# GpSimd's order turned, low halves of weights on VectorE, eight result buffers, x and results laid by query, masks and x loaded first

## The reference

```python
def _L0_xattn_ref(input, memory, mask, w_input, dot_scale):
    input_dot = jnp.einsum('bqd,od->bqo', input, w_input)
    cross_dot = jnp.einsum('bqd,bkd->bqk', input * dot_scale, memory)
    att = input_dot + cross_dot - 1e+30 * mask[:, None, :]
    return jnp.einsum('bqk,bkd->bqd', jax.nn.softmax(att, axis=-1), memory)

def _moe_forward(x, W_router, W_gate, W_up, W_down):
    probs = jax.nn.softmax(jnp.einsum('bsd,ed->bse', x, W_router), axis=-1)
    gates, indices = jax.lax.top_k(probs, 2)
    gates = gates / jnp.sum(gates, axis=-1, keepdims=True)
    # for each expert: y = (silu(x wg) * (x wu)) wd, out += weight * y

x = x + jnp.tanh(g_xattn[0]) * _L0_xattn_ref(_layernorm(x), ctx_1024, mask, w_input, dot_scale)
x = x + jnp.tanh(g_ffn[0]) * _L0_ffn_ref(_layernorm(x), W_router, W_gate, W_up, W_down)
```

## Time and profile before

| | |
|---|---|
| runs | 308.25, 307.16, 308.09 us, median 308.09 |
| profiled execution | 306.35 us, of which the span 304.6 |
| PE busy | 251.2 us, 82% |
| PE weight loads | 205.2 us, 67% |
| VectorE (DVE) | 129.4 us, 42% |
| ScalarE (ACT) | 137.3 us, 45% |
| GpSimd (POOL) | 141.8 us, 47% |
| DMA | 39.27 MB, mean 129 GB/s |

### The profile page before, as it was taken

One profiled execution on the slowest core, in us unless ns is written; L12 is line 12 of the kernel. 1 busy time (PEld: TensorE's weight loads), 2 busy tenths in 40 slices (PEclk: granted clock), 3 DMA queues, 4 the chain that ended last, 5 costly groups with the idle time before them and its releaser, 6 DMA issues.

```text
span 304.6 us, 5760 instructions
## 1 busy us (share of the span) xinstructions
PE 251.2 (82%) x1598; PEld 205.2 (67%) x1599; DVE 129.4 (42%) x421; ACT 137.3 (45%) x295; POOL 141.8 (47%) x243
## 2 busy tenths in 40 slices
PE   5957978999879998798899449739999999999910
PEld 4635758777667776676597438627988888888710
DVE  0252455656535565259446306272334243333205
ACT  2345546555455554555264304412555454545400
POOL 3072432444685666787855885640332323232320
PEclk9997997999989999799979959976999999999975
DMA  5996885778737888479851301321111111114027
GB/s 135 205 194 186 219 201 141 181 171 197 190 109 177 192 214 240 123 208 229 267 171 37 80 8 38 80 64 35 47 43 45 39 49 36 50 39 150 17 73 276
DMA packets 21246, 39.27 MB, mean 129 GB/s; under 512 B 3830, under 2 KB 14134, under 8 KB 21222
## 3 DMA queue, kind: packets, MB, share of 16 engines
q1 hardware_dynamic: 17334, 34.29, 43.7%
q0 software_dynamic: 2560, 3.77, 4.2%
q10 hardware_dynamic: 1328, 0.92, 1.0%
HBM read 32.87 MB, written 6.09 MB: 128 GB/s over the span
## 4 chain that ended last, share of the span: by engine, by line
PE 52%; POOL 15%; DMA 11%; ACT 8%; issue 8%; SPq 3%; DVE 3%; POOLq 0%; DVEq 0%
PE psum L1100 8%; PE psum L997 7%; PE psum L977 7%; PE psum L1078 6%; PE psum L1080 5%; PE psum L1079 5%; DMA maskb<-mask_scaled 5%; PE psum L1089 4%; PE psum L964 4%; DMA x_all<-in_x 4%; POOL slots L528 3%; POOL w_lo L502 3%; ACT probs L650 3%; ACT probsT L616 2%; PE psum L987 2%
## 5 line engine op out<-in xcount | busy, mean ns | idle before, releaser
L583 POOL DMA_INDIRECT results<-y_sb,dest x32 | 30.7, 959 | 65.3 <-DVE dest L897 52.6
L997 PE MATMUL psum<-ctx_sb,probsT 120*100 120x128 f32 (+1 forms) x384 | 51.7, 290 | 0.0
L997 PEld LDWEIGHTS psum<-ctx_sb,probsT 120*100 120x100 f32 (+1 forms) x384 | 47.3, 180 | 0.2 <-issue 0.2
L502 POOL TENSOR_TENSOR w_lo<-w_raw,w_hi 128x512 fp32r<-128x512 f32 x16 | 20.3, 1269 | 50.2 <-ACT w_hi L627 50.0
L977 PE MATMUL psum<-ctxT,qT 128*100 128x512 f32 (+1 forms) x96 | 42.8, 582 | 0.2 <-issue 0.2
L908 DVE SCALAR_TENSOR_TENSOR scores<-probs,row_in,psum 128x512 f32<-128x512 f32 x32 | 23.9, 747 | 38.2 <-ACT probs L682 36.7
L682 ACT ACTIVATE probs<-psum 128x512 f32<-128x512 f32 x32 | 19.1, 597 | 45.7 <-PE psum L1080 40.9
L528 POOL DMA_INDIRECT slots<-pair_rows,slot_i x32 | 33.2, 1036 | 9.8 <-issue 8.5
L1100 PE MATMUL psum<-w_down,hidT 128*128 x256 | 35.8, 285 | 1.0 <-ACT y_sb L694 0.6
L754 DVE CUSTOM_DVE_ANT_0 scores<-psum,maskb 100x1444 f32<-100x1444 f32 x16 | 26.6, 1660 | 18.9 <-PE psum L977 11.7
L1100 PEld LDWEIGHTS psum<-w_down,hidT 128*128 128x128 f32 x256 | 32.7, 200 | 1.8 <-issue 1.8
(11 more groups left out here) (126 smaller groups left out, 371.2 us busy)
## 6 DMA issues: line engine op xcount, KB each, us to landing
ctx_sb<-in_ctx SPq DMA_DIRECT2D x16, 720.0 KB
maskb<-mask_scaled SPq DMA_DIRECT2D x14, 564.1 KB
w_raw<-in_w_experts SPq DMA_DIRECT2D x16, 256.0 KB
row_in<-slots SPq DMA_DIRECT2D x32, 65.0 KB, 1.8
w_down<-in_w_experts SPq DMA_DIRECT2D x4, 512.0 KB
maskb<-in_mask SPq DMA_DIRECT2D x2, 564.1 KB
x<-x_all SPq DMA_DIRECT2D x2, 400.0 KB
ctx_sb<-x SPq DMA_DIRECT2D x1, 800.0 KB, 4.5
```

The costliest lines, as they stand in the source:

```text
L502: nc.gpsimd.tensor_tensor(w_lo[:, b * WC:(b + 1) * WC], w_raw[:, b % 2, :], w_hi[:, b * WC:(b + 1) * WC].bitcast(F32), ALU.subtract).then_ ...
L583: nc.gpsimd.indirect_dma_start(results, bass.IndirectOffsetOnAxis(ap=dest[:, s:s + 1], axis=0), y_sb[:, s, :], None).then_inc(y_stored[s], 16)
L997: last = nc.tensor.matmul(attn_ps[0:Q, 0:D], probsT[0:rows[c], c, :], ctx_sb[0:rows[c], b % RING, c, :], start=(c == 0), stop=(c == CHUNKS ...
```

## The change

- `split_weights` moves from POOL to VectorE, where part b-2 is split in step b ahead of the masked maximum. ScalarE rounds part b-1 in step b, two in step 15, and `w_raw` has four buffers instead of two.
- On POOL the rows of batch 14 come ahead of the gates of batches 12 and 13, and the first result is scattered ahead of the rows of batches 14 and 15.
- `y_sb` and `dest` have eight buffers (`YRING`), and the loop does eight tiles a turn.
- x comes in laid out by query, in groups (0,2), (2,4), (4,8), (8,12), (12,16). Results are laid by query; they are added onto `x_all` itself in four groups of four batches, and stored from there. `x2` is gone, with two stores and a load.
- SP's order: before step 0 there are x to batch 7, context 0 to 2 and the two raw masks. Step b then issues mask b+2, weights b, context b+3; context 3 comes in step 0 behind mask 2, the last two groups of x in steps 1 and 2, and the store of the empty rows in step 3.
- Ten warming matmuls instead of eight at the start.

```diff
-        X_GROUPS = [(0, 1), (1, 4), (4, 8), (8, 12), (12, 16)]
+        X_GROUPS = [(0, 2), (2, 4), (4, 8), (8, 12), (12, 16)]
...
-                wait(sp, w_lo_done, b - 1)
-                sp.dma_start(w_raw[:, b % 2, :], w_experts[:, b * WC:(b + 1) * WC]).then_inc(w_loaded[b % 2], 16)
+                wait(sp, w_lo_done, b - RING + 1)
+                sp.dma_start(w_raw[:, b % RING, :], w_experts[:, b * WC:(b + 1) * WC]).then_inc(w_loaded[b % RING], 16)
...
             load_raw_mask(1)
-            load_weights(0)
+            load_x(2)
             load_ctx(2)
-            load_x(2)
-            load_weights(1)
-            load_ctx(3)
-            load_x(3)
-            sp.wait_ge(empty_done, 1)
-            sp.dma_start(slots[DUMMY:DUMMY + P, :], empty[:, :]).then_inc(empty_stored, 16)
-            load_x(4)
 
             for b in range(B - 2):
                 sp.wait_ge(scores_done, b + 1)
                 if b == 0:
                     sp.wait_ge(mask_stored, 16)
                 load_mask(b + 2)
-                load_weights(b + 2)
-                if b + RING < B:
-                    sp.wait_ge(attn_raw, b + 1)
-                    load_ctx(b + RING)
-                if b == 8:
-                    store_x2(0, 8)
+                if b == 0:
+                    load_ctx(RING - 1)
+                load_weights(b)
+                if 1 <= b and b + RING - 1 < B:
+                    sp.wait_ge(attn_raw, b)
+                    load_ctx(b + RING - 1)
+                if b in (1, 2):
+                    load_x(b + 2)
+                if b == 3:
+                    sp.wait_ge(empty_done, 1)
+                    sp.dma_start(slots[DUMMY:DUMMY + P, :], empty[:, :]).then_inc(empty_stored, 16)
                 if b >= 10:
                     load_down(b - 10)
+            load_weights(B - 2)
+            load_weights(B - 1)
...
+                sp.dma_start(out[m * CUT:(m + 1) * CUT, :, :].rearrange("b q d -> q b d"),
+                             x_all[:, m * CUT:(m + 1) * CUT, :]).then_inc(out_stored, 16)
...
-                if b == B - 1:
-                    split_weights(b)
                 if b in SCATTERS:
...
-                if b < B - 1:
-                    split_weights(b)
...
-            gates(12, 14)
             root2(B - 2)
             normalise2(B - 2)
+            gates(12, 14)
             root2(B - 1)
             normalise2(B - 1)
             pool.wait_ge(placed, 7)
             scatter(12)
             scatter(13)
             gates(14, 16)
-            pool.wait_ge(placed, 8)
-            scatter(14)
-            scatter(15)
...
                 scatter_result(0, n)
+                if n == 0:
+                    pool.wait_ge(placed, 8)
+                    scatter(14)
+                    scatter(15)
...
-                    round_weights(b)
+                    if b >= 1:
+                        round_weights(b - 1)
+                    if b == B - 1:
+                        round_weights(B - 1)
...
+            def split_weights(b):
+                dve.wait_ge(w_hi_done, b + 1)
+                apart(dve)
+                nc.vector.tensor_tensor(w_lo[:, b * WC:(b + 1) * WC], w_raw[:, b % RING, :],
+                                        w_hi[:, b * WC:(b + 1) * WC].bitcast(F32), ALU.subtract).then_inc(w_lo_done, 1)
...
                     attention_gain(b - 1)
+                if b >= 2:
+                    split_weights(b - 2)
+                if b == B:
+                    split_weights(B - 1)
                 if b < B:
                     masked_max(b)
...
-                    wait(dve, y_stored[s], i * 16 + 16 * (k // RING))
-                    nc.vector.tensor_tensor(dest[:, s:s + 1], row_in[:, s, D + 1:D + 2], spare[:, s:s + 1], ALU.min).then_inc(dest_done, 1)
+                    o = k % YRING
+
+                    wait(dve, y_stored[o], i * 16 + 16 * (k // YRING))
+                    nc.vector.tensor_tensor(dest[:, o:o + 1], row_in[:, s, D + 1:D + 2], spare[:, o:o + 1], ALU.min).then_inc(dest_done, 1)
...
+                part = x_all[:, m * CUT:(m + 1) * CUT, :]
                 dve.wait_ge(first_loaded[m], 16)
-                nc.vector.tensor_tensor(x2_sb[:, cut], x2_sb[:, cut], first_sb[:, cut], ALU.add).then_inc(first_added, 1)
+                nc.vector.tensor_tensor(part, part, first_sb[:, m * CUT:(m + 1) * CUT, :], ALU.add).then_inc(first_added, 1)
...
-            keep_warm(8)
+            keep_warm(10)
```

More of the change, by code:

```diff
@@ L27 @@
 RING = 4
-LAG = 3
+YRING = 8
 NEG = -1e30
@@ L215, in build @@
         ctx_loaded = [sem(f"ctx_loaded{s}") for s in range(RING)]
-        w_loaded = [sem(f"w_loaded{s}") for s in range(2)]
+        w_loaded = [sem(f"w_loaded{s}") for s in range(RING)]
         down_loaded = sem("down_loaded")
@@ L284, in build @@
         y_done = sem("y_done")
-        y_stored = [sem(f"y_stored{s}") for s in range(RING)]
+        y_stored = [sem(f"y_stored{s}") for s in range(YRING)]
         first_loaded = [sem(f"first_loaded{m}") for m in range(CUTS)]
@@ L306, in over_tiles @@
                     after(n)
-            with eng.Fori(0, (LOOP_END - LOOP) // RING) as i:
-                for k in range(LOOP, LOOP + RING):
+            with eng.Fori(0, (LOOP_END - LOOP) // YRING) as i:
+                for k in range(LOOP, LOOP + YRING):
                     step(i, k)
@@ L401, in _ @@
             sp.wait_ge(scattered[0], 16 * 2 * PARTS[EARLY_PART][1])
-            for n in range(RING):
-                load_rows(0, n)
-            store_x2(8, B)
-            for n in range(RING, LOOP):
+            for n in range(LOOP):
                 load_rows(0, n)
@@ L410, in _ @@
                         clear_tail(e)
-            with sp.Fori(0, (LOOP_END - LOOP) // RING) as i:
-                for k in range(LOOP, LOOP + RING):
+            with sp.Fori(0, (LOOP_END - LOOP) // YRING) as i:
+                for k in range(LOOP, LOOP + YRING):
                     load_rows(i, k)
@@ L587, in _ @@
                 scatter_result(0, n)
-            with pool.Fori(0, (LOOP_END - LOOP) // RING) as i:
-                for k in range(LOOP, LOOP + RING):
+                if n == 0:
+                    pool.wait_ge(placed, 8)
+                    scatter(14)
+                    scatter(15)
+            with pool.Fori(0, (LOOP_END - LOOP) // YRING) as i:
+                for k in range(LOOP, LOOP + YRING):
                     scatter_result(i, k)
@@ L871, in _ @@
             statistics1(0)
+            statistics1(1)
             dve.wait_ge(scale_loaded, 32)
             evict_ctxT(0)
-            for b in range(1, 4):
-                statistics1(b)
+            statistics1(2)
+            statistics1(3)
             dve.wait_ge(mask_raw, 16)
@@ L917, in add_results @@
             def add_results(m):
-                cut = slice(m * CUT, (m + 1) * CUT)
+                part = x_all[:, m * CUT:(m + 1) * CUT, :]
                 dve.wait_ge(first_loaded[m], 16)
-                nc.vector.tensor_tensor(x2_sb[:, cut], x2_sb[:, cut], first_sb[:, cut], ALU.add).then_inc(first_added, 1)
+                nc.vector.tensor_tensor(part, part, first_sb[:, m * CUT:(m + 1) * CUT, :], ALU.add).then_inc(first_added, 1)
                 dve.wait_ge(second_loaded[m], 16)
                 dve.wait_ge(first_added, m + 1)
-                nc.vector.tensor_tensor(x2_sb[:, cut], x2_sb[:, cut], second_sb[:, cut], ALU.add).then_inc(second_added, 1)
+                nc.vector.tensor_tensor(part, part, second_sb[:, m * CUT:(m + 1) * CUT, :], ALU.add).then_inc(second_added, 1)
             rowT_low(0, 0)
@@ L1092, in down @@
             def down(i, k):
-                n = i * RING + k
+                n = i * YRING + k
                 o = k % 2
@@ L1155 @@
     laid = {
-        "x": a["x"],
+        "x": a["x"].transpose(1, 0, 2),
         "ctx": a["ctx_1024"],
```

100 lines of the change are left out of this document (42 added, 58 removed).

## The result

The kernel after took 288.53 us (median of 4 runs, 287.06 to 290.59), the kernel before beside it 307.62: ratio 0.939, interval 0.932 to 0.946. Predicted were 282.5 us, range 275 to 291. On chip 6 the same two kernels later gave 280.79 and 305.51 us, ratio 0.920 (0.914 to 0.926).

What follows compares the result with a forecast made beforehand. PE was taken to set the pace of undisturbed attention steps, with late POOL, loads and SP's clears adding waits. Terms -3.7 - 11.8 - 7.7 - 1.2 - 1.5 + 1.4 = -24.5 from 306.35 gave 281.9, predicted as 282.5 us, range 275 to 291.

Steps and rivals of the forecast that it cites:

- start, to maximum 4: From the start to maximum 4: new load order brings mask 2 earlier but x late; -3.7 us (0 at worst).
- attention, maximum 4 to 15: Masked maxima 4 to 15: long steps fall back to 8.33 us, 105.6 becomes 93.8; -11.8 us (bounds -14 and -4).
- maximum 15 to tile 0: Last masked maximum to first expert tile: rows 14 ready sooner, 10.0 for 17.72 us; -7.7 us (bounds -5 and -9).
- tile 0 to 7: First seven expert tiles: SP's clears still late, buffers buy nothing before tile 6; -1.2 us (0 to -3).
- loop: Expert loop: turns of eight and fewer waits for stores save time; -1.5 us (0 to -2.5).
- last copy to end: Results by query at the end: additions +1.0 us, last store +0.4, loads nothing; +1.4 us (0.5 to 2.5).
- POOL's wait was the price: Attention: the split's 4.69 us wait for ScalarE makes POOL late; without it long steps fall back to 8.33 us.
- The backlog of step 10: POOL's 10.0 us of work in step 10 makes rows 9 and query 13 late: 1.1 us of PE idling.
- Who is held up: VectorE's new subtraction may hold up POOL's roots and rows, 0.70 us each time; 0.65 charged for two steps.
- The rival of transfers as the bound: Attention steps take 9.1 us for 1.54 MB of transfers, eleven steps lose 8.5, total 291 us; chance 0.15.

Runs made afterwards that it cites:

- experiments 1 and 2: Kernel after with the split back on POOL: at its old place with the wait, 300.88 us (0.982); one part later without it, 287.8 us (0.944).
- clears_late: Kernel after with the index-tail clears issued behind the row load of tile 7 instead of ahead of tile 6's; 290.35 us, ratio 0.937.
- yring4: Kernel after with four result buffers and turns of four tiles instead of eight; 290.16 us, ratio 0.949.
- flat_x2: Kernel after with the old end, x2 to memory and results by batch over 128 partitions; 279.43 us, ratio 0.908.
- experiment 3: Same run as flat_x2: kernel after with the old end, results by batch over 128 partitions; 279.43 us, ratio 0.908.
- clears_two: Kernel after with four of the eight index-tail clears issued from ScalarE's queue; 280.80 us, ratio 0.918.
- tail96: Kernel after with each load of results at the end cut into 96 and 4 queries; 282.69 us, ratio 0.925.
- 6: Kernel after with the fourth part of x issued before the first step instead of behind weights 1; 293.06 us, lowest of four 286.11.
- 8: Kernel after with each mask loaded in two transfers, of 96 and 4 queries; 284.12 us, ratio 0.926.
- 7: Same run as clears_late: kernel after with the index-tail clears behind the row load of tile 7; 290.35 us, ratio 0.937.
- 10: Same run as clears_two: kernel after with four of the eight clears on ScalarE's queue; 280.80 us, ratio 0.918.
- experiment 5: Same run as yring4: kernel after with four result buffers and turns of four instead of eight; 290.16 us, ratio 0.949.

## Why the prediction was right, and where not

The sum by steps, in us against the profiled execution of before (there is no trace of the kernel before from the other chip, so that column carries that chip's own speed too):

| step | predicted | after | other chip |
|---|---|---|---|
| start, to maximum 4 | -3.7 | -3.6 | -0.3 |
| attention, maximum 4 to 15 | -11.8 | -9.4 | -14.0 |
| maximum 15 to tile 0 | -7.7 | -6.6 | -8.0 |
| tile 0 to 7 | -1.2 | -0.2 | -4.7 |
| loop | -1.5 | -2.1 | -1.7 |
| last copy to end | +1.4 | +4.5 | +4.9 |
| sum | -24.5 | -17.3 | -23.8 |

The sum on the other chip is near the forecast by luck: the start gained 3.4 us less than forecast and the end cost 3.5 more, while attention gained 2.2 more and the tiles 3.5 more.

- *POOL's wait was the price.* Shown by experiments 1 and 2, with what stands queued behind it. The split takes 0.69 us on VectorE (0.70 predicted) and delayed no maximum. The backlog of step 10 is there: at 111.49 POOL comes to the roots of batch 9's rows straight from its gates.
- *Who is held up.* I feared it for POOL's roots and rows, and it is so. L438 takes 0.19 us alone, and 0.44 to 0.49 in ten steps in which it starts inside VectorE's subtraction; it then ends with the subtraction. L437 mostly slips in ahead with 0.22 to 0.23 us and was caught twice (0.82 us at 93.10, 0.76 at 118.99). VectorE's own 0.68 to 0.69 never grew. The steps of 8.17 and 8.41 us are those of the undisturbed steps of before, so where POOL has time it costs nothing.
- *Attention.* The seven steps came as said (58.1 us in six of the seven executions named here, 59.8 in `clears_late`). The term as a whole is too small by some 2.5 us on average: 93.8 predicted, 96.2 and 91.6 measured, and 92.1, 96.0, 98.4, 99.1 and 100.5 in `yring4`, `flat_x2`, `clears_two`, `tail96` and `clears_late`, whose attention is the same (`flat_x2` has one store more). What scatters most is the last four steps: 33.5 and 34.0 us at 230 and 226 GB/s, 37.9 at 220, 38.1 at 206, 40.3 and 40.6 at 197, 40.9 at 194, for 7.7 to 8.3 MB each (length times rate). The three longest stand in executions of 283.8, 296.6 and 286.8 us, where the fastest of those kernels took 278.3, 286.1 and 278.9. In the first execution PE waited 2.79 us for context 14, which landed 14.48 us after its issue; share 0.82 there at 206 GB/s, 0.86 at 230 on the other chip. The rival of transfers as the bound is thus true in part, in four steps and some executions. What sets the rate in an execution stays open.
- *Start.* x was there at 42.5 (43 forecast), and the time was met, but the step named one cause where there are two. ScalarE was held 6.71 us by weights 0 (2 to 4 forecast). The new split stands ahead of the maximum on VectorE and waited 5.46 us for ScalarE, where nothing was charged for it, so maximum 2 came at 35.48 instead of near 32. With x in front nothing was gained (6); with weights 0 sooner VectorE waited longer for x (8). That fits the bytes of the whole order as the limit. Maximum 4 stood between 52.3 and 56.8 in the eight executions that share this start, so meeting -3.7 is luck; on the mean of the eight it is -2.
- *End of attention.* 10.0 predicted, 11.14 and 9.73 measured. In the 11.14 PE waited 0.22 us for rows 14, its last wait before tile 0 but a short one; on the other chip none shows.
- *Tile 0 to 7.* SP's clears set it, and the eight buffers bought nothing, as forecast (5, 7, 10). The clears' own duration differs (12.49 and 8.11 us), which is nearly the whole difference of 4.5.
- *Loop.* 1.5 predicted, 2.1 and 1.7 measured; experiment 5 puts 1.5 on buffers and turns together.
- *The failed step is the last.* "The eight additions grow from 400 columns to 512 ... The last store leaves in 512-byte pieces": I charged +1.4 and it was +4.5. Issue of the loads, first and last addition, before (the last stands in the earlier trace rows) and after:

```profile
294.45 1.75 SPq L422 DMA_DIRECT2D ctx_sb<-results  x4
...
297.52 0.58 DVE L921 TENSOR_TENSOR ctx_sb<-ctx_sb 128x400 f32<-128x400 f32 x1 [10.25 <-DMA ctx_sb<-results]
```

```profile
272.64 1.56 SPq L408 DMA_DIRECT2D ctx_sb<-results  x4
...
277.08 0.69 DVE L914 TENSOR_TENSOR x_all<-x_all,ctx_sb 100x512 f32<-100x512 f32 x1 [11.63 <-DMA ctx_sb<-results]
...
283.22 0.69 DVE L917 TENSOR_TENSOR x_all<-x_all,ctx_sb 100x512 f32<-100x512 f32 x1 [0.47 <-DVE x_all L914]
```

The additions were 0.69 us as said (+0.9). The load of the results was put at nothing: the first addition starts 4.44 us after the issue instead of 3.07 (+1.4), and later ones wait again (+1.2). From the end of the last addition to the end of the span it is 3.39 us instead of 2.32, +1.1 where 0.4 was charged for the store. The mechanism (the layout by query costs at the end) was right, its size a third. That the loads over 100 partitions take 0.61 of the DMA engines was seen only in the trace after; that masks go to 100 partitions too could be read before, but no row of before shows such a transfer alone.

The 3.1 us of that step, 2.4 of attention, 1.1 before tile 0, 1.0 in the tiles and 0.1 at the start, less 0.6 of loop, are the 7.2 by which the sum missed (each rounded).

## What to carry to other kernels

Cost an in-order engine's wait by what stands queued behind it, not by the instruction: 1.27 us of subtraction cost 4% only with the wait in front. When a layout changes, price its loads and stores and not only the arithmetic: results over 100 partitions instead of 128 cost 3.4 to 3.9 us where nothing hides it, of which the longer additions were 0.9. And before a miss of 1 to 2% is explained, or one stretch of one trace is used against a theory, run the same kernel again, on another chip too: the same four steps took 33.5 to 40.9 us.

## What was not expected of the hardware

- The same kernel took 288.5 us on one chip and 280.8 on another (0.939 and 0.920 of the kernel before). Eight clears with an address from memory took SP 8.05 to 8.20 us in every kernel on chips 12 and 6 that has all eight on SP, 11.6 to 12.5 in every kernel on chip 15, and 11.45 (before) and 12.49 (after) in the first executions.
- Two queues that load over 100 partitions at once, with the first stores behind them, used 0.61 of the DMA engines at 209 GB/s; over 128, 0.97 at 341.
- Small POOL operations that start beside VectorE's 128x512 subtraction with two SBUF inputs mostly end with it (0.19 became 0.44 to 0.49 us, 0.23 became 0.82); VectorE's own stays at 0.68 to 0.69.
